# Attention over a short context on one core: a one-row bias in the output projection, a smaller statistics block, another order of loads, spreads and tails

## The chip, the cores and the metric

The kernel runs on one core of a Trainium2 chip. The metric is the device time of one execution in microseconds (us); shorter is better. TensorE (PE) multiplies, VectorE (DVE), ScalarE (ACT) and GpSimd (POOL) work on elements, and SyncE (SP) issues DMAs. The engines run unsynchronised and meet only at semaphores.

## The reference

64 batches, 256 queries of width 320, 20 heads of 16, 77 keys of which the last 8 are "image" keys with a softmax and a mask of their own:

```python
q = split(x @ w_q); k = split(ctx[:, :69] @ w_k); v = split(ctx[:, :69] @ w_v)
out_text = softmax(q @ k.T / 4) @ v
mask = ip_mask(bbox)                      # 0 or -10000 for each query and image key
out_ip = softmax(q @ split(ctx[:, 69:] @ w_k_ip).T / 4 + mask) @ split(ctx[:, 69:] @ w_v_ip)
return merge(out_text + out_ip) @ w_out + b_out + x
```

## The kernel before

Every fp32 product is made of rounded high parts and low remainders (hi*hi + hi*lo + lo*hi). ACT writes a high part from PSUM, DVE subtracts it to get the low one.

**Tail stage.** The last 13 context rows of all batches (5 text, 8 image, in 7 tiles `TILES_IN`) are projected first. Their keys lie in `k_tails`, their values in `vt_keep`, to be scaled per batch later (`tail_hi` on ACT, `tail_lo` on DVE, `store_tail` on SP), the first half of the batches in rounds 8 to 14 and the second half in steps -1 and 0 of the main stage.

**Rounds.** The first 64 context rows of four batches (two pairs) make one of 16 rounds `i`. PE transposes two pairs for the next round and multiplies with `w_k` (three products, `ps_k`) and `w_v` (two, `ps_v`). SP, one queue in program order, issues in each round the loads of the context of two pairs (`load_pair`, four DMAs), a store of keys (`store_keys`), four stores of values (`store_values`) and two tail stores. POOL copies tail keys into `k_stage` (L1377). `prepare_main(i)` on DVE makes one part of the constants for the main stage in each round. From round 12 on SP also loads the first x, keys and values of the main stage.

**Main stage.** `sched` runs a step for n = -2 to 65. Step n works on five batches at once: queries of n+2 (E), maxima of the scores of n+1 (A), scores and exponentials of n (Bs), head sums of n-1 (Cs), output projection of n-2 (Ds). The order within a step is written by hand for every engine. On PE: `scores(b, s)` (seven of them, L873, L879) with `sum_heads` (L903), `max_scores` 0 to 4 (L854), `attn_transpose`, `project_out`, `x_transpose` (L818, L819), `stats_transpose` and `project` 0 to 2 between them. `max_scores(a, h4)` overwrites `ps_m` and waits until DVE has reduced the four heads before:

```python
wait(pe, s_mx, b, QUADS, h4)
```

DVE takes for each quad of heads a masked add (L1295) and a reduction (`find_maxima`, L1298). Between them lie `spread_values(0..2)` (L1333), which multiply the values of the batch with the rows that own them, `a_lo` (L1320, L1323), `norm`, `x_lo` (L1270, L1273) and `q_lo`. POOL makes the low part of the probabilities (`rest`, L1402), sums text and image heads (`add_heads`), adds the bias to the residual (`add_bias`, L1422) and the residual to y (`finish`, L1396).

`scores(b, 0)` waits for `q_hi_extra`, whose upper 64 partitions SP copies by a DMA from the queries (`copy_q`, L686), one step ahead. SP's order in a step is `copy_q(b+1)`, `load_x(b+4)`, two stores of y(b-2) (each waits for POOL's `finish`), `load_residual(b)`, `load_values(b+2)` (six DMAs), `load_keys(b+3)` (eight, L665 and L668), and the tail stores in steps 0 and 1.

## Time and profile before

| | |
|---|---|
| median of 3 runs | 1270.41 us (1267.28 to 1271.23) |
| profiled execution: span from the first to the last instruction | 1263.2 us |
| mean granted clock of TensorE | 0.979 |
| busy: PE, DVE, ACT, POOL | 1158.1, 1044.3, 897.6, 904.7 us |
| DMA queues' packets, share of 16 engines' span | 52.9% |

For the profiled execution only the span is given; the median of the runs lies 7.2 us above it, which is the time around the span. A busy share is the union of an engine's instructions over the span. In a row of the windows stand, after the stretch and its length: busy us (and instructions) of PE, of its weight loads, of DVE, ACT and POOL, the granted clock, the DMA share and GB/s. A wait is idle time of an engine in front of an instruction, put down to what ended it.

### The profile page before, as it was taken

The page shows a single profiled execution, that of the slowest core. Times are in us where ns is not written, and L with a number is a line of the kernel's source. Part 1 is how long each engine was busy: PE and PEld are TensorE (multiplying, and loading weights), DVE is VectorE, ACT ScalarE, POOL GpSimd, SP SyncE. Part 2 cuts the span into 40 slices and gives each one's busy share as a digit, 9 for nine tenths or more (in the row PEclk, how much of TensorE's full clock was granted, in tenths as well). Part 3 has the DMA queues.
Part 4 walks back from the last instruction along what each step waited for, and adds up shares of the span by engine and source line. Part 5 has one row for each costly group of instructions (what it writes and reads, how often), then busy time and mean ns, then how long its engine had stood idle before and what let it go on. Part 6 is the DMA issues. An engine that isn't in the chain of part 4 may idle for free.

```text
span 1263.2 us, 34240 instructions
## 1 busy us (share of the span) xinstructions
PE 1158.1 (92%) x12734; PEld 1114.9 (88%) x12734; DVE 1044.3 (83%) x2054; ACT 897.6 (71%) x1923; POOL 904.7 (72%) x1004
## 2 busy tenths in 40 slices
PE   6998887559999999999999999999999999999996
PEld 5898787459999999999999999999999999999985
DVE  5687975669888889888898888888888888898972
ACT  2343343448888888877888888888888888887773
POOL 0111101038889889988988988898898899898896
PEclk9999999779999999999999999999999999999998
DMA  6388887645555545544455554454555555555431
GB/s 173 66 181 168 156 182 149 102 91 111 116 116 120 120 114 121 120 115 114 114 120 120 121 117 115 115 116 115 117 117 115 118 120 117 123 117 114 102 82 61
DMA packets 361460, 151.31 MB, mean 120 GB/s; under 512 B 298640, under 2 KB 350864, under 8 KB 360016
## 3 DMA queue, kind: packets, MB, share of 16 engines
q1 hardware_dynamic: 361296, 149.13, 52.9%
q8 instruction: 103, 1.69, 0.6%
q14 instruction: 61, 0.50, 0.1%
HBM read 88.17 MB, written 39.90 MB: 101 GB/s over the span
## 4 chain that ended last, share of the span: by engine, by line
PE 53%; POOL 11%; DMA 11%; SPq 9%; DVE 6%; issue 5%; ACT 2%; POOLq 0%; ACTq 0%; DVEq 0%
PE ps_a L832 9%; DMA q_hi_extra<-q_hi_lo 8%; PE ps_o L903 8%; PE ps_s L873 7%; PE ps_m L854 6%; PE ps_s L879 6%; PE ps_b L832 6%; POOL prob_lo L1402 6%; PE ps_k L199 2%; PE ps_v L199 2%; SPq L617 2%; SPq L668 2%; POOL y L1396 2%; DMA x_keep<-in_x_dram 2%; PE ps_a L918 2%
## 5 line engine op out<-in xcount | busy, mean ns | idle before, releaser
L1402 POOL TENSOR_TENSOR prob_lo<-prob,prob_hi 128x512 f16<-128x512 f32 (+1 forms) x448 | 506.1, 1148 | 106.0 <-ACT prob_hi L1071 106.0
L873 PE MATMUL ps_s<-q_hi_lo,keys 128*128 128x256 f32 x960 | 248.9, 299 | 44.3 <-DMA q_hi_extra<-q_hi_lo 42.9
L1070 ACT ACTIVATE prob<-ps_s 128x512 f32<-128x512 f32 (+1 forms) x448 | 254.2, 567 | 35.4 <-PE ps_s L879 31.0
L1071 ACT ACTIVATE prob_hi<-ps_s 128x512 f16<-128x512 f32 (+1 forms) x448 | 252.8, 564 | 0.0
L879 PE MATMUL ps_s<-q_hi_extra,keys 128*128 128x256 f32 x960 | 234.1, 281 | 0.3 <-ACT q_hi_extra L1058 0.3
L1298 DVE TENSOR_REDUCE stats<-ps_m 128x8 f32<-128x552 f32 x320 | 231.2, 722 | 0.0
L873 PEld LDWEIGHTS ps_s<-q_hi_lo,keys 128*128 128x128 f32 x960 | 172.6, 190 | 54.1 <-issue 37.4
L903 PE MATMUL ps_o<-values,prob_hi 128*128 128x68 f16 (+7 forms) x3584 | 200.9, 193 | 1.5 <-DVE heads L1312 1.5
L903 PE MATMUL ps_o<-values,prob_lo 128*128 128x68 f16 (+3 forms) x1792 | 190.8, 193 | 0.0
L903 PEld LDWEIGHTS ps_o<-values,prob_hi 128*128 128x128 f16 x3584 | 174.9, 98 | 13.0 <-issue 1.6
L879 PEld LDWEIGHTS ps_s<-q_hi_extra,keys 128*128 128x128 f32 x960 | 173.5, 190 | 0.5 <-ACT q_hi_extra L1058 0.5
L854 PE MATMUL ps_m<-keys,q_hi_lo 128*128 128x308 f32 x640 | 160.9, 333 | 9.5 <-DVE stats L1298 9.4
L903 PEld LDWEIGHTS ps_o<-values,prob_lo 128*128 128x128 f16 x1792 | 166.5, 97 | 0.0
L1333 DVE TENSOR_TENSOR values<-raw_v,own_rows 128x800 f16<-128x800 f16 (+1 forms) x192 | 152.0, 792 | 2.0
L1377 POOL CAST k_stage<-keys 64x520 fp32r<-64x520 f32 x16 | 10.2, 636 | 194.8 <-DMA k_scratch<-k_stage 152.7
L1396 POOL TENSOR_TENSOR y<-y,x_keep 128x320 f32<-128x320 f32 x128 | 126.8, 1010 | 4.3 <-ACT y L1054 4.3
L1410 POOL TENSOR_TENSOR attn<-heads 128x320 f32<-128x320 f32 x128 | 111.6, 872 | 10.0 <-DVE heads L1312 9.4
L1422 POOL TENSOR_TENSOR x_keep<-x_keep,bias 128x640 f32<-128x640 f32 x64 | 105.7, 1652 | 16.5 <-DMA x_keep<-in_x_dram 16.1
L1295 DVE TENSOR_TENSOR ip_masked<-ps_m,stats 128x64 f32<-128x64 f32 x320 | 71.0, 222 | 55.5 <-PE ps_m L854 48.3
L1312 DVE TENSOR_TENSOR heads<-ps_o,inv 128x640 f32<-128x640 f32 x128 | 105.6, 825 | 13.6 <-DVE inv L1308 0.5
L1046 ACT ACTIVATE aT_hi<-ps_a,value_scale 128x512 fp32r<-128x512 f32 x64 | 44.1, 689 | 94.4 <-PE ps_b L919 94.4
L854 PEld LDWEIGHTS ps_m<-keys,q_hi_lo 128*128 128x128 f32 x640 | 97.6, 191 | 11.4 <-issue 9.3
(180 smaller groups left out, 2999.1 us busy)
## 6 DMA issues: line engine op xcount, KB each, us to landing
x_in<-in_x_dram SPq DMA_DIRECT2D x64, 320.0 KB, 3.8
q_hi_extra<-q_hi_lo SPq DMA_DIRECT2D x64, 320.0 KB, 3.4
x_keep<-in_x_dram SPq DMA_DIRECT2D x64, 320.0 KB, 3.2
out_dram<-y SPq DMA_DIRECT2D x128, 160.0 KB, 1.8
k_scratch<-k_stage SPq DMA_DIRECT2D x16, 770.0 KB, 5.8
keys<-k_scratch SPq DMA_DIRECT2D x256, 48.1 KB, 2.1
ctx_in<-in_ctx_dram SPq DMA_DIRECT2D x64, 128.0 KB, 2.8
keys<-k_scratch SPq DMA_DIRECT2D x256, 24.1 KB, 1.9
```

Of the source, the lines that this page charges most:

```text
L832: last = mm(ps, ww if swap else a, a if swap else ww, start=n == 0, stop=n == len(terms) - 1)
L854: last = mm(ps_m[:, t, 0:QUAD], q_hl[third(b)][:, h4, t * P:(t + 1) * P], keys[:, third(b), 0, h4, KOFF:KOFF + QUAD], start=True, stop=True)
L873: mm(ps, keys[:, n, 0, quad, c:c + P], q_hl[n][:, quad, :], start=i == 0, stop=False)
L879: last = mm(ps, keys[:, n, 1, quad, c:c + P], q_ex[q][:, quad, :], start=False, stop=i == len(QPARTS[t]) - 1)
L903: last = mm(o[:, :, oo:oo + w], stat, v[:, :, a:a + w], start=first, stop=False, skip_group_check=True)
L1070: nc.scalar.activation(prob[:, s, 0:w], ps_s[(b[1] + s) % 2][:, 0:w], ACT.Exp)
L1071: nc.scalar.activation(prob_hi[par(b)][:, s, 0:w], ps_s[(b[1] + s) % 2][:, 0:w], ACT.Exp).then_inc(s_hi, 1)
L1298: nc.vector.tensor_reduce(stats[:, :, R_MT + 4 * h4:R_MT + 4 * h4 + 4], ps[:, :, :, 0:T], AX.X, ALU.max).then_inc(s_mx, 1)
L1333: nc.vector.tensor_tensor(v[:, t, :, 2:SLOT], raw_v[par(b)][:].rearrange("p t (o c) -> p t o c", o=1)[:, t] .broadcast_to([P, GTILES[g], S ...
L1396: nc.gpsimd.tensor_tensor(y[par(d)][:, t, :], y[par(d)][:, t, :], x_keep[par(d)][:, t, :], ALU.add).then_inc(s_yr, 1)
L1402: nc.gpsimd.tensor_tensor(prob_lo[par(b)][:, s, 0:w], prob[:, s, 0:w], prob_hi[par(b)][:, s, 0:w], ALU.subtract).then_inc(s_lo, 1)
L1410: nc.gpsimd.tensor_tensor(attn[par(c)][:, t, 0:D].rearrange("p (h c) -> p h c", c=DH), hv[:, :, 0, :], hv[:, :, 1, :], ALU.add)
```

## The change

- **Bias.** `add_bias` on POOL goes. `b_out` is split in two parts which lie as rows 0 and 32 of the third block of `wo_lo`; rows 0 and 32 of a new low tile `aT2[1]` are 1, so that the same eight matmuls of `project_out` add it. The second instruction of `a_hi` writes 128 partitions, not 64.
- **Statistics.** `stats` has 64 columns, not 128; its transposes, and those of the third block of x (64 columns, no longer loaded twice), fill 64 partitions of PSUM. `load_x` is one DMA, not two.
- **Context by GpSimd.** `load_pair` for pairs 4 to 31 is issued by POOL, at the head of its part of the round, not by SP.
- **Order in a round.** Both transposes, then both value products.
- **Batch 0's queries in the last round.** `first(e, a)` replaces steps -2 and -1: x of batch 0 is transposed before the value products of round 15. `copy_q(0)` is issued at the end of SP's rounds, ahead of the keys and values of batch 1. The clearing of `stats` moves to round 12.
- **SP's step.** `copy_q(b+1)`, stores of y(b-3), `load_residual(b-1)`, `load_keys(b+2)`, `load_values(b+2)`, `load_x(b+4)`, one tail store.
- **Spread.** One DVE instruction for all 13 tiles, between `maxima(1)` and `maxima(2)`, in place of three.
- **Tails.** The second half of the tail values, one tile a step, at the end of steps 2 to 8.

```diff
+DL = D - 2 * P
+NSTAT = 64
...
-                    for i in range(NI):
-                        for u in range(2):
-                            if 2 * i + u + 4 < 2 * NI:
-                                sp.wait_ge(s_t, 2 * i + u + 1)
-                                sp.wait_ge(s_sum, 2 * i + u + 1)
-                                load_pair(sp, 2 * i + u + 4)
...
                 def _(pool):
                     for i in range(NI):
+                        for u in range(2):
+                            if 2 * i + u + 4 < 2 * NI:
+                                pool.wait_ge(s_t, 2 * i + u + 1)
+                                pool.wait_ge(s_sum, 2 * i + u + 1)
+                                load_pair(pool, 2 * i + u + 4)
...
+                    copy_q((None, 0, 1))
+                    sp.wait_ge(s_xt, 1)
+                    load_x((None, 2, 1))
                     load_keys((None, 1, 1))
+                    sp.wait_ge(s_xt, 2)
+                    load_x((None, 3, 1))
                     load_values((None, 1, 1))
 
                     def step(sp, b, n):
-                        E, A, Bs, Cs, Ds = has(n)
-                        if A:
+                        if n < 0:
+                            return
+                        if n + 1 < NB:
                             copy_q(off(b, 1))
-                        if n is None or n + 4 < NB:
+                        if 0 <= n - 3 < NB:
+                            store(off(b, -3), 0)
+                            store(off(b, -3), 1)
+                        if 0 <= n - 1 < NB:
+                            load_residual(off(b, -1))
+                        if 3 <= n + 2 < NB:
+                            sp.wait_ge(s_sc, at(b, PAIRS, 0))
+                            load_keys(off(b, 2))
+                        if 2 <= n + 2 < NB:
+                            sp.wait_ge(s_vx, at(b, 1, 1))
+                            load_values(off(b, 2))
+                        if n + 4 < NB:
                             sp.wait_ge(s_xt, at(b, 1, 3))
                             load_x(off(b, 4))
-                        if Ds:
-                            store(off(b, -2), 0)
-                            store(off(b, -2), 1)
-                        if Bs:
-                            load_residual(b)
-                        if n is None or 0 <= n < NB - 2:
-                            sp.wait_ge(s_vx, at(b, 3, 3))
-                            load_values(off(b, 2))
-                        if n is None or 0 <= n < NB - 3:
-                            sp.wait_ge(s_sc, at(b, PAIRS, PAIRS))
-                            load_keys(off(b, 3))
...
-                        for u in range(2):
-                            if i + 1 < NI:
+                        if i + 1 < NI:
+                            for u in range(2):
                                 transposes(2 * (i + 1) + u)
-                            project_values(i, u)
+                            for u in range(2):
+                                project_values(i, u)
...
+                    def first(e, a):
+
+                        x_transpose(a, -2)
+                        for u in range(2):
+                            project_values(NI - 1, u)
+                        for m in range(3):
+                            project(a, m)
+                        x_transpose(e, -1)
+                        max_scores(a, 0)
+                        max_scores(a, 1)
+                        project(e, 0)
+                        max_scores(a, 2)
+                        max_scores(a, 3)
+                        project(e, 1)
+                        max_scores(a, 4)
+                        project(e, 2)
+                        stats_transpose(a)
...
+                        def spread_values():
+
+                            dve.wait_ge(s_vals[par(b)], nth(b, 16 * NVDMA))
+                            wait(dve, s_pv, b, UNITS, -UNITS)
                             nc.vector.tensor_tensor(
-                                v[:, t, :, 2:SLOT],
-                                raw_v[par(b)][:].rearrange("p t (o c) -> p t o c", o=1)[:, t]
-                                .broadcast_to([P, GTILES[g], SLOTS, 2 * DH]),
-                                own_rows[:].rearrange("p t (n c) -> p t n c", n=SLOTS)[:, t], ALU.mult).then_inc(s_vx, 1)
-
-                        if Bs:
-                            spread_values(0)
+                                values[par(b)][:].rearrange("p (t n c) -> p t n c", t=TILES, c=SLOT)[:, :, :, 2:SLOT],
+                                raw_v[par(b)][:].rearrange("p t (o c) -> p t o c", o=1).broadcast_to([P, TILES, SLOTS, 2 * DH]),
+                                own_rows[:].rearrange("p t (n c) -> p t n c", n=SLOTS), ALU.mult).then_inc(s_vx, 1)
...
-                        if Cs:
-                            add_bias()
```

## Rows read from the trace of the kernel before

**Rows 1.** Windows by stage: rounds, passage, first two steps, steady steps.
```profile
47.35:216.87 169.52, 148.01 (x1083) 141.12 (x1083) 129.68 (x257) 66.64 (x148) 19.08 (x27) 0.97 0.81 165
216.87:261.84 44.97, 23.25 (x141) 21.07 (x142) 21.40 (x50) 17.28 (x37) 1.56 (x4) 0.74 0.72 118
261.84:294.10 32.26, 27.43 (x277) 25.72 (x277) 28.46 (x55) 22.91 (x48) 19.88 (x21) 0.89 0.43 84
294.10:1230.59 936.49, 904.45 (x10832) 878.47 (x10829) 826.70 (x1639) 764.82 (x1642) 838.98 (x914) 1.00 0.50 115
```

**Rows 2.** Timeline of ACT: the first exponential of steps 2 and 3.
```profile
294.11 0.58 ACT L1070 ACTIVATE prob<-ps_s 128x512 f32<-128x512 f32 x1
...
308.80 0.58 ACT L1070 ACTIVATE prob<-ps_s 128x512 f32<-128x512 f32 x1
```

**Rows 3.** Waits of the whole span: us in total, times, longest.
```profile
PE ps_s L873 <- DMA q_hi_extra<-q_hi_lo: 42.9, 34, 14.3
```

**Rows 4.** Timeline of one step: SP's queue and the next step's first matmul.
```profile
800.14 1.19 SPq L691 DMA_DIRECT2D out_dram<-y  x2
...
809.38 0.47 SPq L686 DMA_DIRECT2D q_hi_extra<-q_hi_lo  x1
...
812.95 0.36 PE L873 MATMUL ps_s<-q_hi_lo,keys 128*128 128x256 f32 x1 [0.53 <-DMA q_hi_extra<-q_hi_lo]
```

**Rows 5.** Timeline of DVE and PE in one step, around the spreads and `max_scores` 3.
```profile
536.13 1.04 DVE L1333 TENSOR_TENSOR values<-raw_v,own_rows 128x800 f16<-128x800 f16 x1
...
541.23 0.88 DVE L1333 TENSOR_TENSOR values<-raw_v,own_rows 128x800 f16<-128x800 f16 x1
...
542.33 0.72 DVE L1298 TENSOR_REDUCE stats<-ps_m 128x8 f32<-128x552 f32 x1
542.97 0.43 DVE L1333 TENSOR_TENSOR values<-raw_v,own_rows 128x480 f16<-128x480 f16 x1
...
543.87 0.45 PE L854 MATMUL ps_m<-keys,q_hi_lo 128*128 128x308 f32 x2
```

**Rows 6.** Timeline of DVE: two spreads while POOL is idle.
```profile
247.14 0.58 DVE L1333 TENSOR_TENSOR values<-raw_v,own_rows 128x800 f16<-128x800 f16 x1
...
270.69 0.41 DVE L1333 TENSOR_TENSOR values<-raw_v,own_rows 128x480 f16<-128x480 f16 x1
```

**Rows 7.** Timeline of PE: two transposes of x, the first of its third block.
```profile
544.37 0.27 PE L819 MATMUL ps_b<-ident,x_in 128*128 128x128 f32 x1
544.48 0.38 PE L818 MATMUL ps_a<-ident,x_in 128*128 128x128 f32 x2
```

**Rows 8.** Timeline of POOL: the bias add of one step.
```profile
543.64 1.55 POOL L1422 TENSOR_TENSOR x_keep<-x_keep,bias 128x640 f32<-128x640 f32 x1 [0.51 <-DMA x_keep<-in_x_dram]
```

**Rows 9.** Windows by round: PE's rounds 8, 10 and 11.
```profile
133.80:145.80 12.00, 9.33 (x73) 9.07 (x73) 11.53 (x25) 5.03 (x11) 1.17 (x2) 1.00 0.85 154
157.15:166.70 9.55, 9.35 (x72) 9.09 (x72) 6.59 (x15) 4.12 (x11) 0.00 (x0) 1.00 0.94 263
166.70:178.60 11.90, 9.75 (x73) 9.12 (x73) 7.22 (x16) 5.05 (x12) 1.22 (x3) 1.00 0.79 142
```

**Rows 10.** Waits of PE in the rounds.
```profile
PE ps_t L755 <- DMA ctx_in<-in_ctx_dram: 11.3, 7, 4.1
PE ps_k L199 <- DVE ctxT_lo L1122: 11.1, 16, 2.7
```

**Rows 11.** Timeline of SP's queue in a late round: context loads, then value stores.
```profile
207.26 2.50 SPq L192 DMA_DIRECT2D ctx_in<-in_ctx_dram  x4
...
214.33 6.23 SPq L617 DMA_DIRECT2D v_scratch<-v_stage  x4
```

**Rows 12.** Timeline of the passage: last value stores, copy for batch 0, first exponential.
```profile
241.28 6.26 SPq L617 DMA_DIRECT2D v_scratch<-v_stage  x4
...
255.91 0.51 SPq L686 DMA_DIRECT2D q_hi_extra<-q_hi_lo  x1
...
261.84 0.60 ACT L1070 ACTIVATE prob<-ps_s 128x512 f32<-128x512 f32 x1 [10.62 <-PE ps_s L879]
```

More of the change, by code:

```diff
@@ L860, in stats_transpose @@
                         for t in range(NT):
-                            last = nc.tensor.transpose(ps_m[:, 0, t * P:(t + 1) * P], stats[:, t, :], ident[:])
+                            last = nc.tensor.transpose(ps_m[0:NSTAT, 0, t * P:(t + 1) * P], stats[:, t, :], ident[:])
                         last.then_inc(s_et, 1)
@@ new lines, in image_maxima, with first @@
+                    def image_maxima(a):
+                        dve.wait_ge(s_dve, at(a, QUADS, QUADS))
+                        nc.vector.tensor_reduce(stats[:, :, R_MI:R_MI + H], ip_masked[:], AX.X, ALU.max).then_inc(s_ip, 1)
+                    def first(e, a):
+                        x_lo(a)
+                        for u in range(2):
+                            v_lo(2 * (NI - 1) + u)
+                        for m in range(3):
+                            q_lo(a, m)
+                        maxima(a, 0)
+                        x_lo(e)
+                        maxima(a, 1)
+                        maxima(a, 2)
+                        q_lo(e, 0)
+                        maxima(a, 3)
+                        maxima(a, 4)
+                        image_maxima(a)
+                        q_lo(e, 1)
+                        q_lo(e, 2)
```

335 lines of the change are left out of this document (189 added, 146 removed).

## The prediction

> **What bounds the kernel now.** I read the windows by stage first, since the busy shares of the page mix four different stages. They say where the time lies: 169.52 us for fifteen rounds, 44.97 for the passage from round 15 to the first exponential, 32.26 for steps 0 and 1, 936.49 for 61 steady steps [rows 1]. In the steady stage PE is busy 904.45 of 936.49 us, and the mean step is 936.49 / 61 = 15.35 us. The timeline of ACT gives the same step at its best: from 294.11 to 308.80, 14.69 us [rows 2]. Sixteen of the first 60 steady steps took 14.69 to 14.75 us, the rest 14.8 to 16.6; inside all of them PE's matmuls follow each other without a gap, so 14.69 is PE's own length and 0.66 us a step is waiting.
>
> The table of waits names it: 42.9 us in front of `scores(b, 0)`, put down to the copy of the queries [rows 3]. The reader should ask why a copy that is issued a whole step ahead is late. The timeline of SP's queue answers: SP sits in front of the first store of y until POOL's residual add is done (800.14), issues 17 DMAs, the two stores first, and reaches the copy at 809.38; PE, which waits for its landing, resumes 3.57 us later, at 812.95 [rows 4]. The loop is POOL's end of step, SP's queue, copy, PE, and it is a little longer than PE's step. So the bound of the steady stage is PE plus SP's order.
>
> In the rounds the windows show two bounds close together. The fastest round takes 9.55 us with PE busy 9.35 and the DMA engines 0.94 full; a slow one takes 11.90 with PE busy 9.75 and DMA 0.79; and one that carries DVE's constants takes 12.00 with DVE busy 11.53 [rows 9]. PE waited 11.3 us for context and 11.1 us for `ctxT_lo` [rows 10], and SP's queue shows four context loads (2.50 us) and four value stores that hold SP for 6.23 us [rows 11]: SP is full too. In the passage SP is behind all others: the last value stores occupy it until 247.54, then 8 key loads, 6 value loads and 2 of x stand ahead of the copy for batch 0 (255.91), for which the first exponential (261.84) waits 10.62 us [rows 12].
>
> **The change, part by part.** The sum is made against the profiled execution (1263.2 us span); the median of the runs lies 7.2 us above it, and I keep these 7.2.
>
> *SP's step.* `copy_q(b+1)` comes first. Its own conditions (queries of b+1 made, scores of b-1 done) hold about when PE starts the step, so it is issued near the start and lands some 4 us into a step of 14.7. Queued behind it are 18 DMAs. Their waits: the store of y(b-3) waits for an add that POOL ends early in this step; keys wait for the scores of the step before; values wait for the spread, some 7 us in; x waits for `x_transpose(b+2)`, some 9 us in. SP needs about 9.2 us for such a list (800.14 to 809.38 [rows 4]), so it ends before 14.7. The 0.66 us go: 61 x 0.66 = 40.3 us.
>
> *Bias.* POOL loses 1.55 us a step [rows 8] of 838.98 / 61 = 13.75. It is not PE's bound, but it is part of the loop above, and without it POOL stays well under 14.69. PE's count of matmuls is the same. Counted at nothing beyond the 40.3.
>
> *Narrow blocks.* Four transposes a step load 64 columns in place of 128. In the trace a transpose takes its place every 0.11 us (544.37 to 544.48 [rows 7]) and streams the 128 columns of the identity, which the change leaves. If the columns loaded set the pace, it were half of 0.11 for four: 0.22 a step, 14 us in all. I take 0, since in the same trace PE's products of 64 and 128 stationary columns follow at the same pace; 14 goes into the lower end.
>
> *One spread.* This is the part that can cost. Three instructions become one of 2080 elements a partition, all of it ahead of `maxima(2)`. With POOL idle, 800 elements took 0.58 and 480 took 0.41 us [rows 6], which is 0.17 / 320 = 0.53 ns an element, and 2080 would take 0.58 + 1280 x 0.00053 = 1.26 us. Beside POOL's work the three took 1.04, 0.88 and 0.43 [rows 5]; their sum, 2.35 us, is the upper bound. Between the two I scale the quiet value by the middle piece, which stands where the new one will: 1.26 x 0.88 / 0.58 = 1.91 us. What waits for it: the reduction of the third quad ended at 543.05, and the matmul of `max_scores` 3, which it frees, began at 543.87 [rows 5], so there is 0.82 us of room. The spread adds 1.91 - 0.88 = 1.03; PE stalls 0.21 us a step, 61 x 0.21 = 12.8 us. At 1.26 no stall; at 2.35 it is 1.47 - 0.82 = 0.65, 39.7 us. Behind it `norm(0)`, `maxima(3)` and `x_lo` come 0.6 us later than now, since the third piece (0.43) is gone from there; `x_lo` has about that much room. The next step's DVE starts 1.04 earlier, since the first piece is gone too.
>
> The Trainium skill's "SBUF — State Buffer", section "Who interferes with whom", says that a DVE instruction with two SBUF inputs contends with a GpSimd instruction that reads SBUF. The trace agrees: 0.88 and 1.04 us beside POOL's work, 0.58 without. By that rule 1.26 us is to be had only if POOL were idle there, and it isn't.
>
> *Rounds.* SP loses four issues a round (2.50 us [rows 11]); POOL, busy 19.08 of 169.52 us [rows 1], gets them, and issues pairs about a round and a half before their transposes, not behind SP's blocked stores. With both transposes ahead of both value products, `ctxT_lo` has both value products to hide behind, and its 11.1 us go; the 11.3 for context go as well if the transfers are not the bound. DMA work a round is 0.81 x 11.30 = 9.15 us [rows 1]; at the best share seen, 0.94 [rows 9], that is 9.73. So twelve rounds at 9.8 and three with DVE's constants at 11.6 [rows 9]: 152.4 against 169.5, a gain of 17. The ends: 0, and 26 (fifteen at 9.55).
>
> The Trainium skill's "DMA: Bandwidth & Descriptors", section "Issuing engines are not separate DMA queues", speaks against this part: DMAs of all issuers run on the same 16 engines, and another issuer saves only the time to issue. The share of 0.81 to 0.94 bears that out as far as it goes; that outcome is a rival below.
>
> *Passage and first steps.* The copy for batch 0 no longer has 16 issues ahead of it (247.54 to 255.91, 8.4 us [rows 12]), SP arrives less late for want of the context loads, and the tail values no longer stand between the maxima. What remains is a chain: keys' products, one transpose, value products, three projections (94 matmuls at about 0.12 us, between the paces of [rows 5, 7]: 11.3 us), then five maxima of 0.95 (0.23 + 0.72 [rows 5]) with the low parts of x and q between them on DVE (to about 20), statistics, copy to the upper half, scores: 23 to 25 us, and PE's busy time now is 23.25 [rows 1]. I take 24.5 for 44.97: gain 20.5. Steps 0 and 1 lack head sums or output projections; without the tail work in front of them 28.8 for 32.26: gain 3.5. Together 24; ends 10 (only the 8.4 and a little) and 32.
>
> *Costs elsewhere.* Tails in steps 2 to 8 add two DVE instructions where spread 0 (1.04 us) was; the nearest row for one is 0.72, so at most 0.4 a step. Bias splitting adds some short DVE instructions to round 5. I put 2 us for both. The last steps change only in the order of two stores: 0.
>
> Sum: 40.3 - 12.8 + 17 + 24 - 2 = 66.5. Span 1196.7, and with 7.2 around it 1203.9: **1204 us**.
>
> **Rivals.**
> - *The spread eats the steady gain.* One long instruction beside POOL runs at the pace of the pieces: 2.35 us, stall 0.65, step 15.34. For it: spread 0 took 1.04. Against: overheads of two instructions go. 1204 + 39.7 - 12.8 = 1231.
> - *The transfers bound the rounds.* [...] Against: a round of 9.55 at 0.94. 1204 + 17 = 1221.
> - *Better than forecast.* Spread under 1.7 us and rounds at 9.55: 1204 - 12.8 - 9 = 1182; the narrow transposes could add to it.
> - *Slower: context comes late from POOL.* POOL's part of a round also holds the cast that waits for the store of `k_stage` two rounds back. If its loads are issued or served so late that PE waits in each round, with both transposes now in front of both value products nothing covers it. The forecast's mean round is 152.4 / 15 = 10.2 us; the gain elsewhere is lost when rounds take 66.5 / 15 = 4.4 more, 14.6 us. With 6 us of waiting a round: 1204 + 90 = 1294. Against: POOL is idle nine tenths of this stage.
> - *It does nothing.* SP's new order meets another late wait (values behind the spread, x behind the transposes) and the step stays 15.35, while rounds stay DMA bound and the passage gains only 8: 1262 to 1268.
>
> **How the numbers follow.** Forecast 0.49 (1190 to 1217), spread 0.18, transfers 0.14, better 0.10, slower 0.06, nothing 0.03. The range from 1178 to 1240 holds the first four apart from combinations of the second and third (1248) and leaves about 2 in 10. A change within 0.3% (3.8 us) is about what a measurement can't tell from none. Faster: 0.91; the same: 0.03; slower: 0.06.
>
> **What would show it.** The wait of `ps_s` for `q_hi_extra` gone from the table; SP's copy issued within 1 us of a step's start; a step of 14.9 to 15.0 whose one wait is `ps_m` for DVE's `stats`, in front of the third or fourth `max_scores`; one spread of 1.9 us; rounds at a DMA share above 0.9; `ctx_in` no longer waited for; the first exponential near 241 less the rounds' 17, so about 224. Wrong it would be if PE waits in a place where DVE now arrives late (`x_lo`, image maxima), if the spread is above 2.3 us, or if POOL's loads come late.

## The result, and the profile after

The kernel after takes 1210.10 us (median of 4 runs, 1207.89 to 1213.18), the kernel before 1268.85 us (median of 4 runs, 1264.58 to 1271.23). The ratio is 0.954, with a 95% interval of 0.951 to 0.957. The profiled execution took 1210.46 us with a span of 1208.6 us, so 1.9 us lie around the span. One run of e4 (1250.90 us, at a clock of 0.87) and one of the kernel before (1283.65 us, 0.93) were slow at a lower clock and are left out of every time and ratio below.

First the windows by stage, of the kernel after: rounds, passage, steps 0 and 1, steps 2 to 9, steps 2 to 62. They answer to [rows 1]. In a row stand, after the stretch and its length, the busy us (and instructions) of PE, of its weight loads, of DVE, ACT and POOL, the granted clock, the DMA share and GB/s.

```profile
47.96:200.55 152.59, 143.50 (x1082) 140.18 (x1083) 131.96 (x267) 66.00 (x147) 54.40 (x87) 0.98 0.86 180
200.55:235.13 34.58, 19.88 (x142) 17.62 (x140) 16.93 (x41) 10.26 (x24) 1.50 (x4) 0.86 0.75 121
235.13:267.21 32.08, 27.11 (x277) 25.42 (x278) 23.30 (x48) 22.79 (x48) 18.82 (x20) 0.88 0.46 95
267.21:401.00 133.79, 124.12 (x1430) 120.12 (x1427) 113.23 (x214) 108.18 (x231) 95.25 (x112) 0.96 0.49 105
267.21:1174.62 907.41, 896.46 (x10832) 877.90 (x10829) 789.70 (x1530) 773.20 (x1654) 760.52 (x853) 0.99 0.51 115
```

Then the same for steps 10 to 61, first of the kernel after, then of the kernel before.

```profile
401.00:1161.58 760.58, 760.58 (x9263) 747.02 (x9260) 667.82 (x1301) 654.98 (x1406) 653.39 (x729) 1.00 0.52 118
```

```profile
415.81:1216.27 800.46, 773.84 (x9263) 752.01 (x9259) 708.83 (x1405) 654.16 (x1405) 715.91 (x781) 1.00 0.50 116
```

In steps 10 to 61 PE is busy in every microsecond: 760.58 of 760.58. A step is 760.58 / 52 = 14.63 us, and only less work on PE could shorten it. But the eight steps before them take 133.79 us, which is 133.79 - 8 x 14.63 = 16.8 more, with the clock at 0.96. That loss is new: in the kernel before those eight took 121.70. The table below is made from such rows; each stage is counted from one first exponential to the next.

| us | head | 15 rounds | passage | steps 0, 1 | steps 2 to 9 | steps 10 to 61 | step 62 | end | span |
|---|---|---|---|---|---|---|---|---|---|
| before | 47.3 | 169.5 | 45.0 | 32.3 | 121.7 | 800.5 | 14.3 | 32.6 | 1263.2 |
| after | 48.0 | 152.6 | 34.6 | 32.1 | 133.8 | 760.6 | 13.1 | 34.0 | 1208.6 |
| gain | -0.6 | 16.9 | 10.4 | 0.2 | -12.1 | 39.9 | 1.3 | -1.4 | 54.6 |

The waits of PE over the whole span, kernel after (us in total, times, longest); they answer to [rows 3, 10]:

```profile
PE ps_m L876 <- DVE stats L1366: 14.6, 16, 1.5
PE ps_s L895 <- DMA q_hi_extra<-q_hi_lo: 10.1, 1, 10.1
PE ps_k L209 <- DVE ctxT_lo L1185: 9.5, 5, 2.8
```

The wait of `scores` for the copy of the queries is down from 34 times to one, in the passage. (Of the 42.9 us of [rows 3] 14.3 were one wait in the old passage; in the steady steps it was 28.6 us, 33 times.) No row names `ctx_in`. But PE still waits 9.5 us for `ctxT_lo`, 5 times, where it waited 11.1 us, 16 times, before. New at the top is `ps_m`: `max_scores` waits for DVE's maxima. With windows set on the waits, 9.3 us of it (7 times) lie in steps 2 to 9, and PE has no wait at all in steps 10 to 61.

The timeline of SP's queue in one step of the kernel after, and below it the instruction of ACT that the copy had waited for, answer to [rows 4]:

```profile
705.46 0.47 SPq L705 DMA_DIRECT2D q_hi_extra<-q_hi_lo  x1
707.61 1.18 SPq L710 DMA_DIRECT2D out_dram<-y  x2
708.83 0.43 SPq L671 DMA_DIRECT2D x_keep<-in_x_dram  x1
...
716.79 0.39 SPq L667 DMA_DIRECT2D x_in<-in_x_dram  x1
720.08 0.47 SPq L705 DMA_DIRECT2D q_hi_extra<-q_hi_lo  x1
```

```profile
705.07 0.37 ACT L1084 CAST q_hi_lo<-ps_a 64x256 fp32r<-64x256 f32 x1
```

The queue now waits for the queries, not the queries for the queue: the copy goes out at 705.46, as soon as the last high part (705.07 + 0.37) is there, and SP stands idle from 717.2 to 720.08.

The passage (SP's queue and the first exponential, kernel after) answers to [rows 12]:

```profile
210.43 6.04 SPq L635 DMA_DIRECT2D v_scratch<-v_stage  x4
...
223.68 5.98 SPq L635 DMA_DIRECT2D v_scratch<-v_stage  x4
229.71 0.78 SPq L705 DMA_DIRECT2D q_hi_extra<-q_hi_lo  x1
...
235.13 0.60 ACT L1134 ACTIVATE prob<-ps_s 128x512 f32<-128x512 f32 x1 [9.87 <-PE ps_s L901]
```

Not 16 issues stand ahead of the copy for batch 0 any more, but the last four value stores do, which hold SP for 5.98 us.

### The profile page after: what moved, and what is told of

Read it like the earlier page. It is cut to its first block, busy times and chain, and to the rows that moved or that the text cites. A ratio compares the mean times of both kernels' runs of the same rounds, so it can differ in the third digit from the quotient of the medians.

```text
span 1208.6 us, 34030 instructions
## 1 busy us (share of the span) xinstructions
PE 1141.8 (94%) x12734; PEld 1109.6 (92%) x12734; DVE 999.3 (83%) x1937; ACT 898.3 (74%) x1923; POOL 855.6 (71%) x996
## 4 chain that ended last, share of the span: by engine, by line
PE 81%; DVE 7%; issue 2%; ACT 2%; SPq 2%; POOL 2%; DMA 0%; POOLq 0%; DVEq 0%; ACTq 0%
PE ps_a L854 16%; PE ps_o L925 12%; PE ps_b L854 11%; PE ps_s L895 9%; PE ps_s L901 9%; PE ps_m L876 9%; PE ps_k L209 4%; PE ps_v L209 2%; PE ps_a L840 2%; PE ps_a L940 2%; DVE k_stage L1192 1%; PE ps_m L883 1%; PE ps_b L841 1%; PE ps_b L941 1%; SPq L635 1%
## 5 line engine op out<-in xcount | busy, mean ns | idle before, releaser
L1505 POOL TENSOR_TENSOR prob_lo<-prob,prob_hi 128x512 f16<-128x512 f32 (+1 forms) x448 | 542.6, 1222 | 152.1 <-ACT prob_hi L1135 152.0
L1134 ACT ACTIVATE prob<-ps_s 128x512 f32<-128x512 f32 (+1 forms) x448 | 257.3, 574 | 38.9 <-PE ps_s L901 34.2
L1135 ACT ACTIVATE prob_hi<-ps_s 128x512 f16<-128x512 f32 (+1 forms) x448 | 257.0, 574 | 0.0
L925 PEld LDWEIGHTS ps_o<-values,prob_hi 128*128 128x128 f16 x3584 | 174.3, 97 | 13.1 <-issue 1.6
L895 PEld LDWEIGHTS ps_s<-q_hi_lo,keys 128*128 128x128 f32 x960 | 173.4, 191 | 11.9 <-DMA q_hi_extra<-q_hi_lo 10.4
L196 POOL DMA_DIRECT2D ctx_in<-in_ctx_dram x56 | 31.7, 574 | 128.9 <-DVE context_sums L1243 128.9
L1499 POOL TENSOR_TENSOR y<-y,x_keep 128x320 f32<-128x320 f32 x128 | 110.4, 884 | 4.4 <-ACT y L1127 4.4
L1432 DVE TENSOR_TENSOR values<-raw_v,own_rows 128x2080 f16<-128x2080 f16 x64 | 99.0, 1547 | 0.0
L1353 DVE TENSOR_TENSOR q_hi_lo<-ps_a,q_hi_lo 64x256 fp32r<-64x256 f32 x192 | 80.9, 421 | 9.2 <-ACT q_hi_lo L1084 0.9
L1084 ACT CAST q_hi_lo<-ps_a 64x256 fp32r<-64x256 f32 x192 | 70.4, 367 | 22.5 <-PE ps_a L854 7.3
```

The source lines that it names most:

```text
L895: mm(ps, keys[:, n, 0, quad, c:c + P], q_hl[n][:, quad, :], start=i == 0, stop=False)
L925: last = mm(o[:, :, oo:oo + w], stat, v[:, :, a:a + w], start=first, stop=False, skip_group_check=True)
L1134: nc.scalar.activation(prob[:, s, 0:w], ps_s[(b[1] + s) % 2][:, 0:w], ACT.Exp)
L1135: nc.scalar.activation(prob_hi[par(b)][:, s, 0:w], ps_s[(b[1] + s) % 2][:, 0:w], ACT.Exp).then_inc(s_hi, 1)
L1499: nc.gpsimd.tensor_tensor(y[par(d)][:, t, :], y[par(d)][:, t, :], x_keep[par(d)][:, t, :], ALU.add).then_inc(s_yr, 1)
L1505: nc.gpsimd.tensor_tensor(prob_lo[par(b)][:, s, 0:w], prob[:, s, 0:w], prob_hi[par(b)][:, s, 0:w], ALU.subtract).then_inc(s_lo, 1)
```

## The experiments

Twelve kernels ran. Each profiled span is cut into the same stages:

| us | 15 rounds | passage | steps 0, 1 | steps 2 to 9 | steps 10 to 61 (mean step) | span |
|---|---|---|---|---|---|---|
| after | 152.6 | 34.6 | 32.1 | 133.8 | 760.6 (14.63) | 1208.6 |
| e1 tail_lo a step later | 151.3 | 36.9 | 32.1 | 125.1 | 761.6 (14.65) | 1201.3 |
| e2 copy before stores | 152.7 | 24.7 | 34.6 | 133.8 | 760.4 (14.62) | 1203.2 |
| e3 old queue order | 154.1 | 33.2 | 33.1 | 129.9 | 790.6 (15.20) | 1237.4 |
| e4 context by SP | 162.4 | 35.1 | 32.1 | 133.8 | 760.5 (14.63) | 1216.8 |
| e5 three spreads | 151.4 | 35.3 | 31.4 | 134.1 | 760.5 (14.63) | 1208.4 |
| e6 old round order | 160.8 | 32.8 | 32.0 | 130.7 | 760.6 (14.63) | 1210.6 |
| e7 before, new queue order | 167.3 | 44.5 | 34.1 | 119.5 | 784.4 (15.09) | 1248.1 |
| e8 pieces, copy first | 152.6 | 24.7 | 37.4 | 117.1 | 760.5 (14.63) | 1188.0 |
| e9 add on new residual | 154.2 | 33.4 | 33.0 | 129.2 | 761.4 (14.64) | 1208.3 |
| e10 add on old residual | 152.4 | 34.8 | 32.0 | 133.8 | 760.6 (14.63) | 1210.4 |
| e11 pieces alone | 152.4 | 34.6 | 32.0 | 117.1 | 760.5 (14.63) | 1192.0 |
| e12 e7 without bias add | 170.0 | 44.9 | 32.9 | 117.6 | 764.5 (14.70) | 1223.8 |

**The late tails (e1, e11).** The timelines of DVE and of ACT at the end of a step of the kernel after, one of steps 2 to 9:

```profile
329.55 0.42 DVE L1353 TENSOR_TENSOR q_hi_lo<-ps_a,q_hi_lo 64x256 fp32r<-64x256 f32 x1
330.97 1.89 DVE L1209 SCALAR_TENSOR_TENSOR vt_late<-vt_keep,tail_unscale,vt_late 32x320 f16<-32x320 f32 x2 [1.00 <-ACT vt_late L1059]
332.89 0.22 DVE L1363 TENSOR_TENSOR ip_masked<-ps_m,stats 128x64 f32<-128x64 f32 x1
333.03 0.72 DVE L1366 TENSOR_REDUCE stats<-ps_m 128x8 f32<-128x552 f32 x1
```

```profile
329.31 1.04 ACT L1092 CAST q_hi_extra<-q_hi_extra 64x1024 fp32r<-64x1024 f32 x1
330.38 1.15 ACT L1059 ACTIVATE vt_late<-vt_keep,tail_unscale 32x320 f16<-32x320 f32 x2
```

And PE's timeline, the `max_scores` behind them:

```profile
333.90 0.52 PE L876 MATMUL ps_m<-keys,q_hi_lo 128*128 128x308 f32 x2 [1.52 <-DVE stats L1366]
```

DVE waits 1.00 us for the high part that ACT makes in the same step, spends 1.89 us on two low parts, and the first maxima of the next step start 2.9 us after the last `q_lo` (in a quiet step, at 706.57, 0.5 us after it); `max_scores` 1 waits for them. e1 takes the wait away by making the low parts one step later:

```diff
-                        if 0 <= n - 2 < len(TILES_IN):
-                            tail_lo(1, n - 2)
+                        if 0 <= n - 3 < len(TILES_IN):
+                            tail_lo(1, n - 3)
...
-                        if 0 <= n - 3 < len(TILES_IN):
-                            store_tail(1, n - 3)
+                        if 0 <= n - 4 < len(TILES_IN):
+                            store_tail(1, n - 4)
```

> The changed kernel with the low parts of the late tail values made by DVE one step later (end of steps 3 to 9) and stored one step later; the work is the same, only DVE no longer reaches it before ACT has made the high part. Steps 2 to 9 took 133.8 us in the changed kernel, 16.8 more than eight quiet steps of 14.62. Theory A (DVE waits for ACT in order, the next step's maxima queue behind it): about half or more of the 16.8 us goes, time 1195 to 1202. Rival B (the two DVE instructions themselves, 0.8 to 1.0 us each, are too long for the slack): the steps stay at 16 to 18 us, 1208 to 1212. Rival C (ACT's part delays the next step): no change either, and PE's waits in front of the attention transposes or projections, not in front of max_scores.

Measured: 1203.50 us, ratio 0.952 (0.949 to 0.954). Steps 2 to 9 fell from 133.8 to 125.1, about half of the loss, and the time came out a little above the 1195 to 1202 us of theory A. The two low parts still stand together in front of the maxima, without a wait and at 2.03 us for the two:

```profile
343.13 2.03 DVE L1209 SCALAR_TENSOR_TENSOR vt_late<-vt_keep,tail_unscale,vt_late 32x320 f16<-32x320 f32 x2
```

So the other half, 125.1 - 117.05 (e11, below) = 8.0 us, is the length of the pair. e11 takes one head group a step instead of a tile of two, the low part a step behind its high part and the store a step behind that; thirteen steps carry one instruction on DVE (0.96 us) where seven carried one or two:

```diff
+                PIECES = [(u, o) for u in range(len(TILES_IN)) for o in range(WIDTHS[u])]
...
-                        if 0 <= n - 2 < len(TILES_IN):
-                            tail_hi(1, n - 2)
+                        if 0 <= n - 2 < len(PIECES):
+                            tail_hi_piece(*PIECES[n - 2])
...
-                        if 0 <= n - 2 < len(TILES_IN):
-                            tail_lo(1, n - 2)
+                        if 0 <= n - 3 < len(PIECES):
+                            tail_lo_piece(*PIECES[n - 3])
```

> The kernel after with the late tails in pieces of one instruction a step alone, the passage as in the kernel after. If pieces and the earlier copy add up as the stages of e8 say: passage 34.6, steps 0 and 1 32.1, steps 2 to 9 117.1 us, so the span is 1208.6 - 16.7 = 1191.9 and the time about 1194. Rival: the tails' stores start later by a step or more and meet nothing, so steps 0 and 1 change too (as in e8, where they took 37.4 us against 34.6 in e2): then the time is 1196 to 1198.

Measured: 1194.45 us, ratio 0.943 (0.942 to 0.945), the value of the sum. The window of steps 2 to 9, kernel e11:

```profile
267.38:384.43 117.05, 117.05 (x1430) 114.98 (x1427) 109.08 (x208) 105.33 (x225) 101.92 (x112) 1.00 0.53 118
```

PE is busy throughout and its clock is 1.00, against 124.12 of 133.79 us and 0.96 in the kernel after. The late tails cost 133.79 - 117.05 = 16.7 us, of which 9.7 are idle time of PE (133.79 - 124.12). For the rest the windows of two stretches of the kernel after, from 300 and from 316 us, give a reading:

```profile
300.00:316.00 16.00, 15.73 (x159) 15.32 (x160) 12.54 (x25) 11.61 (x25) 10.96 (x14) 0.89 0.45 92
316.00:334.00 18.00, 16.01 (x201) 15.25 (x201) 16.16 (x31) 15.72 (x35) 13.07 (x16) 1.00 0.53 122
```

The clock was 0.89 in three such stretches and 1.00 in those between, so in some steps that follow a wait PE works for a while at its lower level, and its busy time grows by what the idle time doesn't show. How the 16.7 us split between waits and clock differs from kernel to kernel: e5, below, waits longer there (13.3 us for `stats`, 9.3 in the kernel after), has a clock of 0.99 and takes 134.1 us. The window of e9 (below) for these steps, which hold the same tails, shows what the clock cost in the kernel after:

```profile
268.91:398.13 129.22, 119.48 (x1430) 115.49 (x1427) 112.74 (x214) 108.25 (x230) 107.73 (x120) 1.00 0.50 109
```

PE's idle time is the same there (9.74 us against 9.67), its clock is 1.00, and the steps take 129.22 us. So of the 16.7 us about 4.6 come with the lower clock, 4.1 with the wait that e1 takes away (129.22 - 125.09) and 8.0 with the length of the pair. This split is read from one execution of each. Why the same tails brought the lower clock in one kernel and not in the other stays open.

**The passage (e2, e8).** e2 issues the copy for batch 0, x and the keys ahead of the last value stores:

```diff
                         if i == 15:
+                            copy_q((None, 0, 1))
+                            sp.wait_ge(s_xt, 1)
+                            load_x((None, 2, 1))
+                            load_keys((None, 1, 1))
                             load_values((None, 0, 1))
...
-                    copy_q((None, 0, 1))
-                    sp.wait_ge(s_xt, 1)
-                    load_x((None, 2, 1))
-                    load_keys((None, 1, 1))
```

> The changed kernel with the copy of batch 0's queries, x of batch 2 and the keys of batch 1 issued at the head of SP's round 15, before the values of batch 0 and the last key and value stores. In the changed kernel the copy was issued at 229.7 us although its queries were ready at 213.5, and PE waited 10.1 us for it. Theory (SP's queue bounds the passage): the first exponential comes 8 to 10 us earlier, at 225 to 227, and the time is 1200 to 1204 if the first steps don't give it back. Rival (the values of batch 0 or the DMA rings, filled by the value stores, are the next bound): the first exponential comes earlier but steps 0 and 1 grow by as much, 1207 to 1211.

Measured: 1202.75 us, ratio 0.951 (0.948 to 0.953). The passage is 24.74 us, PE's clock in it 1.00. But steps 0 and 1 took 2.6 us more, 34.6: PE now waits there once for the copy of batch 1's queries, which goes out at 239.59, behind the last value stores (228.44 to 234.47), x and 6 value loads. The waits of PE in steps 0 and 1, kernel e2, have this row, and those of the kernel after have none for `q_hi_extra`:

```profile
PE ps_s L895 <- DMA q_hi_extra<-q_hi_lo: 3.7, 1, 3.7
```

SP's copy in the passage of e2, which answers to the row at 229.71 above, and the window of the passage:

```profile
219.15 0.64 SPq L705 DMA_DIRECT2D q_hi_extra<-q_hi_lo  x1
...
228.44 3.97 SPq L635 DMA_DIRECT2D v_scratch<-v_stage  x2
```

```profile
201.81:226.55 24.74, 19.43 (x142) 17.31 (x140) 16.93 (x41) 10.25 (x25) 1.49 (x4) 1.00 0.77 124
```

e8 is e2's edit and e11's in one kernel.

> A version meant to be better than both: the changed kernel with the copy of batch 0's queries first (as in the experiment on the passage) and the late tails in 13 pieces, one DVE, one ACT instruction and one store a step in steps 2 to 16, DVE a step behind ACT. Steps 2 to 10 held 16.8 us of excess in the changed kernel and 9.2 with DVE a step later. Theory (what is left is DVE's own time in one place, and half of it fits): 13 steps with 0 to 0.3 us of excess each, together 0 to 4 us; passage 24.7; time 1187 to 1193. Rival (any tail work in front of maxima 0 delays PE by about its length): 13 x 0.55 to 0.8, 7 to 10 us, 1194 to 1200.

Measured: 1186.97 us, ratio 0.937 (0.935 to 0.940), the fastest of all, below both the kernel before and the kernel after. Steps 0 and 1 took 37.4 us, so that of the 9.8 us won in the passage 5.3 are given back there. Up to step 2 its program is that of e2, where they took 34.6: 2.8 us is what one execution differs from another there (PE waits 4.5 us for the copy and not 3.7, the clock is 0.86 and not 0.90).

**The queue order (e3).** The step's SP part of the kernel before, in the kernel after:

```diff
                             copy_q(off(b, 1))
-                        if 0 <= n - 3 < NB:
-                            store(off(b, -3), 0)
-                            store(off(b, -3), 1)
-                        if 0 <= n - 1 < NB:
-                            load_residual(off(b, -1))
...
                         if n + 4 < NB:
                             sp.wait_ge(s_xt, at(b, 1, 3))
                             load_x(off(b, 4))
+                        if 0 <= n - 2 < NB:
+                            store(off(b, -2), 0)
+                            store(off(b, -2), 1)
+                        if n < NB:
+                            load_residual(b)
...
```

> The changed kernel with SP's step order of the kernel before (copy, x, stores of y(b-2), residual(b), values, keys(b+3)). Theory (the copy was late because SP sat in front of the store of y until POOL had finished, and 15 issues followed): the wait for q_hi_extra comes back and the mean steady step goes from 14.62 to 15.1 to 15.35, time 1230 to 1250. Rival (POOL's relief from the bias add already broke the loop, since POOL finishes 1.6 us earlier in a step): steady steps stay at 14.62 to 14.75, time 1208 to 1216.

Measured: 1238.78 us, ratio 0.979 (0.977 to 0.982). The mean step is 15.20 and the wait for the copy is back, in the waits of PE, kernel e3:

```profile
PE ps_s L893 <- DMA q_hi_extra<-q_hi_lo: 33.6, 30, 8.7
```

The order is worth 790.6 - 760.6 = 30.0 us in 52 steps, 0.58 a step, once the bias is off POOL.

**The order alone, and the bias (e7, e9, e10, e12).** e7 is the kernel before with the new order of SP's step (e3's diff the other way round) and the last two stores behind the loop.

> The kernel before with one part of the change alone, SP's new order in a step (bias still added by POOL, three spreads, tails in steps -1 and 0). Theory (the order alone breaks the loop): steady steps fall from 15.35 to 14.70 to 14.75, time 1225 to 1234. Rival (POOL with the bias add still closes a loop, since the residual is now loaded a step later, shortly before POOL adds the bias to it): steady steps of 14.9 to 15.3, time 1235 to 1262.

Measured: 1254.08 us, ratio 0.990 (0.987 to 0.993). The mean step in steps 10 to 61 is 15.09, where it was 800.46 / 52 = 15.39: of the 0.69 us above 14.70 less than half went. The waits of POOL and PE, kernel e7, and one bias add on POOL's timeline:

```profile
POOL x_keep L1424 <- DMA x_keep<-in_x_dram: 74.3, 62, 3.5
...
PE ps_a L920 <- POOL attn L1414: 18.4, 21, 2.3
```

```profile
812.26 1.57 POOL L1424 TENSOR_TENSOR x_keep<-x_keep,bias 128x640 f32<-128x640 f32 x1 [1.51 <-DMA x_keep<-in_x_dram]
```

The new order loads the residual of batch b-1 in step b, behind the stores of y that wait for POOL's add of the step before. e7 still has POOL's bias add, which wants that residual in the same step: it waits 74.3 us in all, 1.2 a step (16.1 in all in the kernel before), and `attn_transpose` waits for POOL. One loop has taken the place of another. Two kernels asked whether POOL's length or that lateness does it: the kernel after with one more add on POOL at the old place of the bias add, on the residual of b-1 (e9) or of b-2 (e10):

```diff
                             rest(1)
+                        if Cs:                     # e10: if Ds
+                            same_again(c)          # e10: same_again(d)
...
+                        def same_again(w):
+                            pool.wait_ge(s_xk[par(w)], nth(w, 16))
+                            nc.gpsimd.tensor_tensor(x_keep[par(w)][:], x_keep[par(w)][:], x_keep[par(w)][:],
+                                                    ALU.add).then_inc(s_xb, 1)
```

> The kernel after, with one more POOL add of the size and at the place of the old bias add (after rest(1)), on the residual of batch b-1 that was loaded in this same step, as in e7; it adds the residual to itself, so the output holds twice the residual. Theory A (the residual lands just before POOL wants it, and POOL's end of step is late by that): steps 10 to 61 at about 15.08 us as in e7, PE waits for attn, time about 1210 + 61 x 0.45 = 1237. Theory B (it is only POOL's length, 1.55 us more a step): the same 1237 here, and in e10 too. Theory C (the add's 1.55 us are hidden with the new queue order, and what e7 lost came from the rest of the old kernel): 14.63 us a step, 1210.

> The same add of the same length at the same place of POOL's order, but on the residual of batch b-2, which was loaded a whole step before, so that POOL waits for no transfer; the output again holds twice the residual. Theory A: POOL's 1.55 us are hidden, 14.63 us a step, about 1210. Theory B: 15.08 us a step, about 1237, as e9. Theory C: 1210. A value between (14.75 to 14.95, 1218 to 1230) would mean that both the length and the lateness count.

Measured: 1212.61 us, ratio 0.958 (0.956 to 0.960), for e9 and 1211.47 us, 0.957 (0.954 to 0.959), for e10, against 0.954 (0.951 to 0.957) of the kernel after. Neither cost anything that can be told from no change; the mean steps are 14.64 and 14.63. So theories A and B fell as they were told, and an add at this place is hidden in the kernel after. But e9 is not e7's case: its add took 1.30 us and not 1.57, and POOL waited for the residual 17.9 us in all and not 74.3. Over steps 10 to 61 its residual is issued 0.4 us before `rest(0)` starts (median; 0.1 after it in e7) and its add starts 3.3 us after (3.6 in e7). The copy of the mask into the narrower `stats` took 0.20 against 0.32. e12 is e7 with the bias add left out:

```diff
                             if t == 0:
-                                pool.wait_ge(s_xb, at(d, 1, 1))
+                                pool.wait_ge(s_xk[par(d)], nth(d, 16))
...
-                        if Cs:
-                            add_bias()
```

> e7 (the kernel before with the new queue order) and the bias add of POOL left out, so the output lacks the bias. In e7 POOL waited 1.2 us a step for the residual and then spent 1.57 us on the bias add, and PE waited for attn; in e9 the same lateness with an add of 1.30 us cost nothing. If the bias add closes that loop in e7: PE's own 14.70 us a step, steps 10 to 61 at about 764 us instead of 784.4, span about 1248 - 20 - 4 = 1224, time about 1230, a ratio of 0.970. Rival (the three spreads, the wide statistics and the double x loads of the old kernel hold the step at 15.09): no change against e7, time about 1254, 0.990. In between (15.0 to 14.8) would leave a part to each.

Measured: 1224.98 us, ratio 0.966 (0.963 to 0.968). The window of steps 10 to 61, kernel e12:

```profile
414.53:1179.04 764.51, 764.51 (x9263) 751.14 (x9260) 704.85 (x1405) 653.30 (x1406) 645.46 (x729) 1.00 0.54 122
```

PE has no gap, and its step is 14.70. So in the kernel before the queue order gives 800.5 - 784.4 = 16.1 us of these steps and, once it is there, the bias add's going gives 19.9 more. With the rest of the change in place an add of 1.30 us there costs nothing (e9); one of 1.57 us was not tried. e12 takes away the wait for the residual and the add together, so that it doesn't say which of the two closed e7's loop. POOL's loop in e7 is longer than PE's step by a few tenths of a us, and the change shortens it in more than one place; which of e9's shorter pieces tips it wasn't tried one by one.

**The spread (e5).** Three spreads at their old places, in the kernel after:

```diff
+                        if Bs:
+                            spread_values(0)
                         if A:
                             maxima(a, 0)
...
-                            spread_values()
+                            spread_values(1)
                         if A:
                             maxima(a, 2)
+                        if Bs:
+                            spread_values(2)
```

> The changed kernel with the values spread in three DVE instructions at the three old places. In the changed kernel the one spread takes 1.57 us and PE does not wait behind it. Theory (the merge was neither needed nor harmful in a steady step, PE being the bound): steady steps stay at 14.62 to 14.70; steps 2 to 9, where the tail work now meets the first spread in front of maxima 0, grow by up to 1 us each; time 1208 to 1219. Rival (DVE is close enough to its limit that 0.8 us more a step is felt): steady steps of 14.8 to 15.2, time 1220 to 1245.

Measured: 1211.00 us, ratio 0.956 (0.953 to 0.959), the same as the kernel after. The three pieces took 0.92, 0.92 and 0.47 us, so 2.31 a step, the one instruction 1.55 (from the page's groups, first of e5, then of the kernel after):

```profile
L1435 DVE TENSOR_TENSOR values<-raw_v,own_rows 128x800 f16<-128x800 f16 x128 | 117.7, 920 | 2.0
L1435 DVE TENSOR_TENSOR values<-raw_v,own_rows 128x480 f16<-128x480 f16 x64 | 30.1, 470 | 0.0
```

```profile
L1432 DVE TENSOR_TENSOR values<-raw_v,own_rows 128x2080 f16<-128x2080 f16 x64 | 99.0, 1547 | 0.0
```

DVE saves 0.76 us a step and PE gains nothing from it, since it doesn't wait for DVE there.

**The rounds (e4, e6).** e4 gives the context loads back to SP, at their old place; e6 keeps POOL's loads and takes back the order on PE (shown below), ACT and DVE:

```diff
                     for i in range(NI):
+                        for u in range(2):
+                            if 2 * i + u + 4 < 2 * NI:
+                                sp.wait_ge(s_t, 2 * i + u + 1)
+                                sp.wait_ge(s_sum, 2 * i + u + 1)
+                                load_pair(sp, 2 * i + u + 4)
                         load_main(i)
```

> The changed kernel with the context loads of the rounds issued by SP again, all else as changed. Fifteen rounds took 152.6 us in the changed kernel and 169.5 before. Theory (SP's full queue made the context late): rounds grow by 8 to 15 us and the passage by 0 to 5 since SP ends later, time 1218 to 1230. Rival (the rounds gained by the order of transposes and value products, the transfers being the bound): rounds grow by under 4 us, 1209 to 1214.

```diff
                             for u in range(2):
                                 transposes(2 * (i + 1) + u)
-                            for u in range(2):
                                 project_values(i, u)
```

> The changed kernel with the old order in a round (transpose, value products, transpose, value products, and ACT and DVE to match), context still issued by GpSimd. Rounds took 152.6 us in the changed kernel, 162.4 with SP issuing the context and 169.5 before. Theory (the two causes add, the order hides ctxT_lo, some 0.5 to 0.8 us a round): rounds of 158 to 165 us, time 1215 to 1223, and PE waits for ctxT_lo in front of ps_k in every round. Rival (the transfers set the pace once POOL issues the context): rounds of 151 to 155, time 1208 to 1213.

Measured: e4 1218.62 us, ratio 0.964 (0.960 to 0.968), rounds of 162.4 us; e6 1214.65 us, 0.959 (0.956 to 0.961), rounds of 160.8. Taken back by itself each half costs 8 to 10 us: 9.8 the issuer, 8.2 the order (their sum, 18.0, is above 16.9; rounds of one and the same program took 151.3 to 154.2 in the other kernels). The waits of PE in the rounds, first of e4, then of e6, answer to [rows 10]:

```profile
PE ps_t L781 <- DMA ctx_in<-in_ctx_dram: 8.9, 7, 2.8
PE ps_k L209 <- DVE ctxT_lo L1190: 4.0, 4, 2.0
```

```profile
PE ps_k L209 <- DVE ctxT_lo L1183: 15.8, 16, 3.1
```

Without POOL's loads PE waits for context, without the new order for `ctxT_lo` 16 times, each as the prediction had read its half. The window of e4's rounds adds something:

```profile
48.47:210.88 162.41, 149.85 (x1082) 144.70 (x1083) 131.75 (x268) 66.57 (x147) 19.95 (x27) 0.95 0.83 171
```

Against the kernel after PE is idle 12.56 us and not 9.09; the other 6.35 of the 9.82 us are busy time, at a clock of 0.95 and not 0.98.

## Why the prediction was right, and where it was not

The forecast was 1204 us, and 1210.10 was measured; the mechanism and the sign held, and the terms of the sum against the span of the kernel before compare so:

| term, us of gain | forecast | measured |
|---|---|---|
| queue order, with the bias off POOL; steps 2 to 62 | 40.3 | 45.9 |
| one spread | -12.8 | 0 |
| rounds | 17 | 16.9 |
| passage, steps 0 and 1 | 24 | 10.6 |
| tails and other costs | -2 | -16.8 |
| head and end | 0 | -2.0 |
| sum | 66.5 | 54.6 |

*SP's step.* Right in place: the wait is gone and the copy goes out as soon as its queries are there. (The prediction read all 42.9 us of [rows 3] as the steady step's; 28.6 were. The 0.66 a step came from the steps' lengths and doesn't rest on it.) The 45.9 us are 936.49 - 907.41 = 29.1 plus the 16.8 that the tails took back. They are more than 40.3 since PE's own step fell as well, from 14.70 (e12) to 14.63: 0.075 x 61 = 4.6 us. The prediction put the narrow blocks at nothing, with 14 as the bound. Counted from the start of one matmul to the start of the next over steps 10 to 61 of both traces, the two transposes of the statistics fell from 0.173 to 0.143 us a step, those of x stayed at 0.57, and the 24 matmuls of `project` fell from 2.91 to 2.85. So the narrow transposes are less than half of it; why `project` got faster wasn't tried.

*Bias at nothing.* This held for the kernel as a whole (e9, e10, with an add of 1.30 us) and not for the step as it was told: the order alone gave 0.31 us of the 0.69 (steps 10 to 61), while it moved the residual to just before POOL's bias add (e7), and with the old kernel's other work on POOL the order needs the bias gone (e12). The prediction saw that POOL's add is part of the loop, but not that the new order loads the residual behind POOL's last add.

*One spread.* The term that was mis-sized upward. Its 1.91 us were measured as 1.55 and its stall of 0.21 as none: steps 10 to 61 have PE busy throughout, with one spread or three. I had scaled the whole by a piece that lies beside POOL's work. The Trainium skill's "SBUF — State Buffer", section "Who interferes with whom", says that a DVE instruction with two SBUF inputs contends with a GpSimd instruction that reads SBUF. The trace of the kernel after agrees in the main: six of the 64 spreads had POOL busy beside them for under 0.3 us and took 1.27 to 1.37 us, near the quiet estimate of 1.26; the median, with POOL busy throughout, is 1.56, and the longest 2.02. What it costs, 0.3 us, is half of what the scaling gave.

*Rounds.* The sum is right to 0.2 us, and both halves count (e4, e6). Its terms are not: twelve rounds of 9.8 us at a DMA share of 0.94 and three of 11.6 stood there, and the rounds went from 9.08, with PE busy throughout, to 12.37, at a share of 0.86 over all; and of the 11.1 us for `ctxT_lo`, which were to go, 9.5 stayed. That 152.4 stood for 152.59 is in part luck. The rival "the transfers bound the rounds" did not come true. The Trainium skill's "DMA: Bandwidth & Descriptors", section "Issuing engines are not separate DMA queues", says that another issuer saves only the time on the sequencer, usually small. Here it is not small: SP is held for 6.04 us by four value stores in the kernel after (6.23 before, [rows 11]), the context loads stood behind them, and moving them gave 9.8 us against e4 while the DMA share rose from 0.83 to 0.86.

*Passage and first steps.* Mis-sized. Of 20.5 us in the passage 10.4 came. The step that failed is "the copy for batch 0 no longer has 16 issues ahead of it": those issues went, the last four value stores stayed ahead (5.98 us), and behind them the landing. e2 takes them away and the passage is 24.74 us, where 24.5 stood. Steps 0 and 1 kept 32.1 us where 28.8 stood; in no run were they under 31.4. PE is idle there for 5.0 us, for maxima and once for keys, and the clock is 0.88. With the copy first they are longer (34.6 in e2, 37.4 in e8), since the last stores still have to go through the same queue and now stand ahead of the copy for batch 1, for which PE waits 3.7 and 4.5 us. No run changed that by itself.

*Costs elsewhere.* Mis-sized, and the largest error: 2 us were put for 16.8. The nearest row gave 0.72 us for a low part on 32 partitions; alone it takes 0.96, two take 1.89 to 2.03. The trace of the kernel before already had two of 1.26 and 1.35 us, in step 0 (263.25 and 266.60). And it was counted by length alone: its wait for ACT in the same step (1.00 us), its place in front of the next step's first maxima, and the stretches at a lower clock behind PE's waits were left out. e1 shows the first (4.1 us), e9 beside the kernel after the last (4.6), e11 all of it together.

*Around the span.* I took 7.2 us, the median of the runs less the span of the profiled one. It is 1.9 (1210.46 and 1208.6 of one execution). The other 5.3 were the spread between executions, and they hid as much of the errors: 66.5 - 54.6 = 11.9 too much gain, less 5.3, leaves the 6.6 us between 1203.9 and 1210.46.

So the total is nearer than its terms: the spread and SP's step gave 18.4 us more than was forecast, the passage, the tails and the ends 30.2 less, and the 5.3 took up a part of the rest. The mechanism of the steady step was right; that the time lies within 7 us of 1204 is in part luck.

## What to carry to other kernels

When a wait is removed by reordering a queue, follow every DMA that moves, and ask of each whose instruction now finds it late: e7 kept less than half of the gain, with POOL waiting 1.2 us a step for a residual that was moved one step back. A small instruction that waits for another engine at the end of a step costs its wait and its length; one short piece a step cost nothing where a pair a step cost 2 us. Forecast each gain by the wait that it removes, and look for that wait afterwards: in the rounds the sum came true with one of the two waits still there. Where a chain through a queue ends a stage, list what is still ahead in the queue, stores too.

## What the runs showed of the hardware

- Short waits of PE (at most 1.5 us each for `stats` in steps 2 to 9) can come with a lower clock: 0.89 in three stretches of the kernel after. It is no rule of these runs: e5 waited longer in the same places and showed it once, by its windows, and e9, with the same waits, not at all.
- A long DVE instruction on two SBUF inputs was cheaper here than its pieces beside POOL's work: 1.55 us for 2080 elements against 0.92 + 0.92 + 0.47 = 2.31 us for the same in three.
- POOL took 0.57 us for each context load that it issued, and the loads landed after 5.8 us in the median, as these rows of the page's groups and of its DMA issues of the kernel after show. It was hidden: PE has no wait for `ctx_in` there, and the loads issued from 59.0 us on are transposed from 72.2 us on.

```profile
L196 POOL DMA_DIRECT2D ctx_in<-in_ctx_dram x56 | 31.7, 574 | 128.9 <-DVE context_sums L1243 128.9
...
ctx_in<-in_ctx_dram POOLq DMA_DIRECT2D x56, 128.0 KB, 5.8
```
